# A two-pass graph kernel whose TensorE increments move from the last matmul to a drain behind it

## What is computed

```python
def _L0_gnn_ref(x, edge_index, edge_attr, W1, b1, W2, b2, ...):
    msg = jax.nn.relu(x[src] + edge_attr)
    agg = jax.ops.segment_sum(msg, dst, num_segments=x.shape[0])
    h = x + (x + agg)
    f = jax.nn.gelu(_bn(h, ...bn1) @ W1.T + b1, approximate=False) @ W2.T + b2
    return _bn(h + f, ...bn2)

def _L1_gnn_ref(node_embeddings, edge_index, edge_embeddings, W1m, b1m, ...):
    h = jax.nn.gelu((node_embeddings[src] + edge_embeddings) @ W1m + b1m, approximate=False)
    agg = segment_sum(h @ W2m + b2m, dst) / maximum(degree, 1.0)
    u = jax.nn.gelu(agg @ W1u + b1u, approximate=False) @ W2u + b2u
    return _layer_norm(node_embeddings + u, gamma, beta)

x = _layernorm(x + _L0_gnn_ref(x, edge_index, edge_attr_256, ...), axis=-1)
x = _layernorm(x + _L1_gnn_ref(x, edge_index, edge_attr_256, ...), axis=-1)
```

## Time and profile before

| | before |
|---|---|
| median of 3 runs | 2640.95 us |
| span of the profiled execution | 2670.8 us |
| PE busy (matmul) | 2066.5 us, 77% |
| POOL busy | 1639.4 us, 61% |
| DVE busy | 1471.0 us, 55% |
| ACT busy | 1309.5 us, 49% |
| first pass, steady stretch | 300 to 1200 us: 75 groups |
| second pass, steady stretch | 1400 to 2560 us: 92 groups |

### The profile page before, as it was taken

One profiled execution on the slowest core, in us unless ns is written; L12 is line 12 of the kernel. 1 busy time (PEld: TensorE's weight loads), 2 busy tenths in 40 slices (PEclk: granted clock), 3 DMA queues, 4 the chain that ended last, 5 costly groups with the idle time before them and its releaser, 6 DMA issues.

```text
span 2670.8 us, 37695 instructions
## 1 busy us (share of the span) xinstructions
PE 2066.5 (77%) x9234; PEld 1690.3 (63%) x9234; DVE 1471.0 (55%) x3208; ACT 1309.5 (49%) x2691; POOL 1639.4 (61%) x1689
## 2 busy tenths in 40 slices
PE   4787777777777787887657888788788788878878
PEld 3566666666566566666446666666676666666766
DVE  3355555454554544545435665666666566666666
ACT  4555455554555554555324454454454454444453
POOL 6666666666666666664366666666666566666650
PEclk9898988889989888889868888898988988988897
DMA  6788778878788788887446666666666666666661
GB/s 215 247 268 258 257 257 258 271 248 275 252 263 265 252 262 264 261 264 248 146 144 174 180 184 179 178 191 179 180 186 181 177 178 178 189 182 177 186 187 49
DMA packets 347352, 566.93 MB, mean 212 GB/s; under 512 B 48104, under 2 KB 213604, under 8 KB 347284
## 3 DMA queue, kind: packets, MB, share of 16 engines
q1 hardware_dynamic: 267098, 347.29, 42.1%
q0 software_dynamic: 79824, 218.08, 26.9%
q10 hardware_dynamic: 362, 0.85, 0.1%
HBM read 499.54 MB, written 66.49 MB: 212 GB/s over the span
## 4 chain that ended last, share of the span: by engine, by line
PE 29%; another core or an unknown queue 23%; issue 19%; DVE 13%; ACT 11%; DVEq 4%; ACTq 1%; DMA 0%; POOL 0%; POOLq 0%; SPq 0%
PE bank L1051 11%; PE bank L993 5%; DVE m_lo L1312 3%; PE bank L1018 3%; ACT bank L735 3%; ACT m_all L739 3%; PE bank L1068 3%; PE bank L963 2%; DVEq L1265 2%; PE bank L890 2%; DVE sel L1246 1%; PE bank L975 1%; DVE bank L1306 1%; ACT bank L768 1%
## 5 line engine op out<-in xcount | busy, mean ns | idle before, releaser
L564 POOL DMA_INDIRECT m_all<-y_scratch,src_u x831 | 808.4, 973 | 492.4 <-DVE bank L1306 259.9
L564 POOL DMA_INDIRECT m_all<-in_x,src_p x816 | 807.0, 989 | 417.0 <-issue 210.8
L1051 PE MATMUL bank<-w1m_sb,e_all 128*128 128x256 f32 x2076 | 607.4, 437 | 221.7 <-DVE m_lo L1312 125.7
L1051 PEld LDWEIGHTS bank<-w1m_sb,e_all 128*128 128x128 f32 x2076 | 425.2, 217 | 312.8 <-issue 129.4
L993 PE MATMUL bank<-m_all,sel 128*128 128x257 f32 x1664 | 496.1, 430 | 138.7 <-ACT m_all L739 110.0
L1306 DVE TENSOR_TENSOR bank<-bank,m_all 128x512 f32<-128x512 f32 x416 | 289.8, 697 | 454.6 <-remote 306.8
L993 PEld LDWEIGHTS bank<-m_all,sel 128*128 128x128 f32 x1664 | 345.7, 214 | 240.2 <-ACT m_all L739 125.8
L1018 PE MATMUL bank<-w1m_sb,ez 128*128 128x256 f32 x1248 | 357.1, 412 | 141.6 <-issue 74.8
L767 ACT ACTIVATE m_hi<-bank 128x512 fp32r<-128x512 f32 x416 | 248.3, 597 | 320.4 <-DVE bank L1306 112.2
L1018 PEld LDWEIGHTS bank<-w1m_sb,ez 128*128 128x128 f32 x1248 | 242.7, 204 | 191.7 <-issue 162.3
L1068 PE MATMUL bank<-m_lo,sel 128*128 128x256 f32 x831 | 302.4, 385 | 36.9 <-issue 24.1
(11 more groups left out here) (176 smaller groups left out, 2063.0 us busy)
## 6 DMA issues: line engine op xcount, KB each, us to landing
e_all<-in_edge SPq DMA_DIRECT2D x416, 256.0 KB
e_all<-in_edgeT SPq DMA_DIRECT2D x208, 256.0 KB
ez<-in_edgeT SPq DMA_DIRECT2D x104, 384.0 KB
z_scratch<-zc SPq DMA_DIRECT2D x104, 384.0 KB
e_all<-z_scratch SPq DMA_DIRECT2D x104, 256.0 KB
e_all<-in_edgeT SPq DMA_DIRECT2D x104, 128.0 KB
e_all<-z_scratch SPq DMA_DIRECT2D x104, 128.0 KB
m_all<-y_scratch,src_u POOLq DMA_INDIRECT x831
```

The costliest lines, as they stand in the source:

```text
L564: pool.indirect_dma_start(out=m_sb[n % ROUND][:, t, :], out_offset=None, in_=table, in_offset=bass.IndirectOffsetOnAxis(ap=sources(g, u), ...
L1051: last = pe.matmul(z_bank(s)[:, t * D:(t + 1) * D], eT_sb[s % ERING][:, k, t * P:(t + 1) * P], w1m_sb[:, k, :], start=(k == 0), stop=(k == ...
```

## The change

Five places of TensorE's program change in one way. Before, the last matmul of the section carried the increment. Now it carries none; a drain of TensorE's queue stands behind it and carries it. Nothing else moves, no wait changes, and no instruction changes its place. The dense stages of the nodes (`node_a`, `node_b`) keep their increments on the matmuls.

```diff
@@ ahead @@
                 for k in range(KD):
-                    last = pe.matmul(ahead_bank[a // 2][:, a % 2 * D:(a % 2 + 1) * D],
+                    pe.matmul(ahead_bank[a // 2][:, a % 2 * D:(a % 2 + 1) * D],
                                      ez_sb[q % 2][:, k, a * P:(a + 1) * P],
                                      w1m_sb[:, k, :], start=(k == 0), stop=(k == KD - 1))
                 if a:
-                    last.then_inc(z_ahead if a == AHEAD - 1 else z_ahead0, 1)
+                    pe.drain().then_inc(z_ahead if a == AHEAD - 1 else z_ahead0, 1)
@@ sums @@
-                last.then_inc(pair_summed, 1)
+                pe.drain().then_inc(pair_summed, 1)
@@ turn_group @@
-                turn_sums(bank[2 if first else q % 2], sum_n[q % 2], first == 0).then_inc(sum_turned, 1)
+                turn_sums(bank[2 if first else q % 2], sum_n[q % 2], first == 0)
+                pe.drain().then_inc(sum_turned, 1)
@@ product @@
-                last.then_inc(z_made, 1)
+                pe.drain().then_inc(z_made, 1)
```

## The result

The changed kernel takes **2894.7 us** (median of 4 runs, 2875 to 2904), the kernel before 2641.3 us (4 runs, 2635 to 2650): a ratio of 1.095 [1.092, 1.098], 253 us slower. The forecast was 56 us faster. The time lies inside the range of 2400 to 3100, on the other side of no change. The profiled execution's span grew from 2670.8 to 2895.3 us.

A forecast was written before the change was run, and what follows sets the result against it. No single engine was the bound; late matmul increments stalled TensorE and its readers. With drains TensorE bounds: 591 + 242 + 35 = 868 against 900, and 1148 against 1160; over the passes -43 and -13, 2641 - 56 = 2585 us, range 2400 to 3100.

The forecast's parts named there:

- The increments of the matmuls arrive late while gathers run: Kernel before, both passes: matmul-carried increments are held back some us; two consumers started 4.5 and 3.7 us late.
- The drain's increment arrives at once: Behind five TensorE sections: prompt drains remove the held-back increments, TensorE becomes the bound, -56 us; chance 0.58.
- the drain's own end: 0.05 us: Part of each drain's cost: it ends some 0.05 us after the last matmul, read from one drain at the end.
- The constant of a drain, 0.46 us: Each TensorE drain: tail, own end, fetch, restart and register steps together 0.46 us, bounds 0.16 and 0.60.
- TensorE's 591 + 242: First pass, 300 to 1200 us: matmuls at full clock 591 us plus 525 drains at 0.46, 242 us.
- Waits that stay, 35 and 35 us: TensorE's remaining waits in the stretches of the first and second pass: taken as 4%, 35 us each.
- The clock: TensorE's matmuls summed at full clock in both passes, where 0.90 and 0.89 was granted before.
- the clock doesn't come back: Rival: 1560 short pauses keep TensorE's matmuls as slow as now, 274 us more, 2860 us; chance 0.08.
- Late whoever sends it: Rival: the way to the semaphore holds increments, so drains only add time; 2938 to 3359, say 3150 us; chance 0.13.
- The dense stages hold the next drain: Rival: drains wait for 216 increments kept on dense-stage matmuls, 1 to 3 us each; say 3000 us; chance 0.11.
- The rule of the skill: Attach increments to the matmul, which fire at completion; one apart belongs on a drain. First half speaks against the change.

The follow-up runs named there:

- chip C: Kernel before and changed kernel, both unchanged, run on another chip: 2204.7 and 2491.8 us, ratio 1.132 [1.129, 1.135].
- chips B to D: Three chips where the kernel before, unchanged, took 2198.8, 2203.2 and 2198.7 us; with plain copies for gathers 0.859, 0.860 and 0.859 of that.
- A and E: Two chips where the kernel before, unchanged, took 2645.6 and 2644.0 us.
- chip E: Kernel before, unchanged: 2644.0 us; with 64-byte gathers 2649.0 us, 1.003; with plain copies for gathers 1889.7 us, 0.7155.

## Why the prediction was wrong

**The increments of the matmuls arrive late while gathers run:** right, and measured as such: in the kernel before two in three of those that can be followed are late, by 3.0 us in the mean of these; without gathers or with plain copies all come after 14 ns. Not foreseen: only some chips do it.

**The drain's increment arrives at once:** right in the words and wrong in what was meant. Behind the end of a drain nothing is seen to be late (in the rows at 1033 us POOL starts 0.27 us after it). But it was tacitly taken that the drain ends when the last matmul does. The step that failed is "the drain's own end: 0.05 us", in which waiting for late completions stands at nothing. Its source was the one drain at the end of the program, which stands where no gather runs. The prediction had itself shown with the earlier trace rows that without gathers all is prompt, and so the row could not speak for the hot path. In 86 of 100 cases it is 0.02 us, but over all it is 0.19 us a drain: 302 us in place of the 78 that 1560 times 0.05 allow. These 224 us more alone turn -56 into a loss.

**The constant of a drain, 0.46 us:** right: 0.47 us by the table (245 us for 525 drains, 346 us for 736), 0.40 by the pair without gathers. What the price was set against was the weaker part: even with no drain held, TensorE's 591 + 242 left only 67 us of 900 for all else.

**Waits that stay, 35 and 35 us:** too high, 7 and 9. TensorE, once the bound, waits for hardly anything.

**The clock:** the forecast let it return in full. It rose from 0.90 to 0.92 and from 0.89 to 0.97, and 48 and 34 us of slow matmuls beyond the restart stayed. The rival "the clock doesn't come back" had put 274 us on it; about 100 us on the two whole passes came true (48 x 1200/900 + 34 x 1290/1160 = 102). On chip C and without gathers the drains leave the clock at 0.99, so it isn't the pauses of 0.3 to 0.5 us that lower it; what lowers it is the longer pauses of the held drains, going by what differs. That was not tried by itself.

**The rivals.** *Late whoever sends it* foresaw the side, but not its way: no drain's increment is late, and 2938 was its lower end. *The dense stages hold the next drain* foresaw the form, drains of some us, and named the wrong holder: a drain is held as often with a dense stage's increment since the last drain (10 of 100) as without (12 of 100), and behind all five sections, not behind the dense stages. What was missing is a blend of both: any drain waits for late completions, whichever section they belong to. Nothing in the trace of before gave its size, but the earlier trace rows bounded one such wait at 3.7 to 4.5 us, beside a constant of 0.46.

**The rule of the skill.** The prediction set the Trainium skill's PSUM — Partial Sum Buffer, section Engine vs sequencer instructions, against the trace: attach the increment to the matmul. On chips B to D the trace agrees with it to the letter (14 ns). On A and E it doesn't while gathers run; following it is still cheaper by 253 us than the drain.

## What to carry to other kernels

A drain behind TensorE's matmuls isn't a way to make a semaphore prompt: it costs 0.40 us each once TensorE is the bound, and it waits for the same late completion that delayed the semaphore, with the whole engine instead of one reader. Measure a sequencer operation's price where it will stand, not where the trace happens to have one: the drain in the earlier trace rows stood in a stretch without the disturbance. And if "remote" stands in the waits of a program on one core, take away the suspect (here the gathers) before working around the symptom: on chip E, 754 us hang on the gather instructions.

## What the runs showed of the hardware

- While GpSimd issues gathers, completions of TensorE's matmuls are reported late on some chips: some two in three of the increments that can be followed, 3.0 us in the mean of the late ones. With plain copies, or none, they come after 14 ns. Increments of DVE and ACT are not late where they can be followed (some 10 ns).
- On the same chips, and only while gathers run, the profile also lacks the records of about half of the semaphore updates of DVE and ACT. A wait that reads "remote" or "issue" there can be one whose record is lacking. Counting each increment up to the next record, whichever it belongs to, would call over a third of DVE's and ACT's late, which they are not.
- The same program takes 2200 us on three chips and 2644 us on two others, with no difference left once the gathers are gone (1888 to 1892 us on B, C, D and E with plain copies). The kernel before isn't slow on A and E for its own sake; a verdict in us from one chip needn't hold on the next. Here the sign was the same on both kinds.
- A drain of TensorE ends 0.02 us after the last matmul where nothing is late, and on chip C the next matmul starts 0.06 to 0.3 us after that in 92 of 100 cases (0.15 us in the mean of these).
- A gather of 64 bytes a row takes GpSimd as long as one of 1024 (0.97 us).
- Open: what a gather does to TensorE's completions, why only on some chips, and whether fewer or sparser gathers would do it less. Open too is whether what loses the records also holds the completions: both show on the same chips and with the same instruction, no execution without the recording is on record, and no run tells the two apart.
